# Expert layer of an eight-layer transformer: capped logits in four column strips, expert choice from them, and more gathered rows added ahead

## What is computed

```python
logits = x @ wg.T
logits = SOFTCAP * jnp.tanh(logits / SOFTCAP)          # SOFTCAP = 30
probs = jax.nn.softmax(logits, axis=-1)
topk_vals, topk_ids = jax.lax.top_k(probs, TOP_K)      # TOP_K = 2
topk_w = topk_vals / jnp.sum(topk_vals, axis=-1, keepdims=True)
route = zeros.at[arange(T)[:, None], topk_ids].set(topk_w)
h1 = jnp.einsum('th,eih->tei', x, w1);  h3 = jnp.einsum('th,eih->tei', x, w3)
out = jnp.einsum('teh,te->th', einsum('tei,ehi->teh', gelu(h1) * h3, w2), route)
```

## Time and profile before

| | |
|---|---|
| median of 3 runs | 1297.35 us (1296.9 to 1300.2) |
| the profiled execution | 1297.6 us, its span 1295.9 us (1.7 us lie around it) |
| busy shares | PE 90%, DVE 63%, ACT 51%, POOL 40% |
| mean granted TensorE clock | 0.935 |
| head, first logit product to first product of block 0 | 773.0 to 800.5 us |
| loop and spreading | 800.5 to 1022.6 us |
| DVE's last instruction of the layer | starts at 1027.9 us |

### The profile page before, as it was taken

The page is one execution under the profiler, slowest core; times in us unless marked ns, Lnnn a source line. Parts: engine busy times, 40 slices in busy tenths (PEclk is TensorE's granted clock), DMA queues, the critical chain, the costliest instruction groups (busy, mean ns, idle before and its releaser), DMA issues. The chain is left out here.

```text
span 1295.9 us, 23722 instructions
## 1 busy us (share of the span) xinstructions
PE 1161.5 (90%) x8549; PEld 882.3 (68%) x8549; DVE 816.3 (63%) x1970; ACT 664.2 (51%) x1543; POOL 513.2 (40%) x527
## 2 busy tenths in 40 slices
PE   3999999999999779777999974999999589999877
PEld 2777777777777527555677763888888467777545
DVE  6655555645644344676787755766666567777686
ACT  3344544455554332225667641666666157766575
POOL 1355654556555300028788863010000541461132
PEclk9999999999999879787999975999999879999997
DMA  7000000000000115130011024999995360000000
GB/s 194 1 14 12 3 11 13 1 13 1 1 1 1 36 42 159 39 97 23 24 33 38 12 93 142 374 379 378 366 333 181 101 174 14 16 12 2 2 8 22
DMA packets 81459, 109.03 MB, mean 84 GB/s; under 512 B 9664, under 2 KB 57168, under 8 KB 81344
## 3 DMA queue, kind: packets, MB, share of 16 engines
q1 hardware_dynamic: 79568, 102.93, 24.5%
q0 software_dynamic: 1776, 4.59, 1.2%
HBM read 102.91 MB, written 4.59 MB: 83 GB/s over the span
## 5 line engine op out<-in xcount | busy, mean ns | idle before, releaser
L907 POOL TENSOR_SCALAR a_arena<-a_arena 112x487 f32<-112x487 f32 x128 | 192.7, 1517 | 175.4 <-DVE a_arena L1124 175.4
L1213 ACT ACTIVATE a_arena<-banks,a_arena 112x487 f32<-112x487 f32 x128 | 84.3, 663 | 192.0 <-DVE a_arena L1118 192.0
L1118 DVE TENSOR_REDUCE a_arena<-banks 112x2 f32<-112x974 f32 x64 | 75.0, 1172 | 100.0 <-PE banks L995 100.0
L397 POOL TENSOR_TENSOR a_arena<-a_arena 112x375 f32<-112x375 f32 x128 | 114.5, 920 | 24.2 <-ACT a_arena L704 24.0
L513 PE MATMUL banks<-ident,a_arena 112*126 112x112 f32 x768 | 106.2, 275 | 12.8 <-POOL a_arena L397 10.3
L513 PEld LDWEIGHTS banks<-ident,a_arena 112*126 112x126 f32 x768 | 77.6, 144 | 47.3 <-issue 27.3
L2094 DVE TENSOR_TENSOR f_up_low<-f_arena,f_up_high 128x1024 fp32r<-128x1024 f32 x80 | 95.8, 1219 | 9.6 <-ACT f_up_high L2266 9.6
L712 ACT COPY a_arena<-banks 126x336 f32<-126x336 f32 x128 | 56.1, 438 | 72.8 <-PE banks L513 72.8
L2266 ACT CAST f_up_high<-f_arena 128x1024 fp32r<-128x1024 f32 x84 | 84.2, 1056 | 8.4 <-DMA f_arena<-in_L_ffn_w1T 7.8
L2150 POOL DMA_INDIRECT f_arena<-f_rows,f_arena x21 | 20.2, 961 | 171.1 <-PE banks L2188 156.8
L93 PE MATMUL banks<-a_wv_high,a_kvT_high 128*122 128x512 f32 (+1 forms) x224 | 85.6, 382 | 1.9 <-DVE a_kT_low L1070 1.9
(11 more groups left out here) (345 smaller groups left out, 2914.9 us busy)
## 6 DMA issues: line engine op xcount, KB each, us to landing
f_arena<-in_L_ffn_w1T SPq DMA_DIRECT2D x42, 512.0 KB, 7.8
f_arena<-in_L_ffn_w3T SPq DMA_DIRECT2D x42, 512.0 KB, 8.9
f_arena<-in_L_ffn_w2T SPq DMA_DIRECT2D x21, 1024.0 KB, 9.7
a_arena<-in_ctxT SPq DMA_DIRECT2D x24, 375.0 KB, 5.5
a_arena<-in_ctx SPq DMA_DIRECT2D x16, 375.0 KB
f_y<-f_arena SPq DMA_DIRECT2D x19, 128.0 KB, 7.6
a_arena<-in_L_xattn_Wkv SPq DMA_DIRECT2D x2, 1024.0 KB, 10.0
a_arena<-in_fside_BxSxS SPq DMA_DIRECT2D x8, 164.1 KB, 2.3
```

What stands on the lines that cost most here:

```text
L397: op = pool.tensor_tensor(z, z, gp[u], ALU.mult)
L907: pool.tensor_scalar(z, z, inv[:, n % 4, s:s + 1], None, ALU.mult).then_inc(p_ready, 1)
L1118: dve.tensor_reduce(negmax[:, n % 4, :], banks[0:T, 0:2, 0:KEYS], AX, ALU.max, negate=True).then_inc(max_ready, 1)
L1213: act.activation(prob[n % PR][s][:, 0:KEYS], banks[0:T, s, 0:KEYS], ACT.Exp, bias=negmax[:, n % 4, s:s + 1], accum_out=total[:, n % 4, s:s ...
```

## The change

The gate weights become the stationary operand, padded with zeros to 32 columns; 224 rows of x move past them in each of four column strips of PE, so that logits stand with experts on partitions. Tanh works on these strips (128 x 224). Eight transposes of 32 x 112 bring the capped logits back into four PSUM banks (32 columns for each group, 8 of them used). The two largest are found from the capped logits. The weights come from their difference: with e = exp(second - first), they are 1 / (1 + e) and e / (1 + e); they are made behind the token numbers. In the return four groups are added ahead instead of two, and `gathered(b + 4)` stands behind `returned(b)` and ahead of the statistics.

```diff
-        self.psL = ps[0:T, 0:B * E].rearrange("p (b e) -> p b e", e=E)
+        self.psL = ps[:, 0:R // 4]
+        self.capped = turned[0:T, :, 0:2 * STRIP].rearrange("t q (h e) -> t q h e", h=2)[:, :, :, 0:E]
...
+        pool.memset(self.wg[:, :, E:STRIP], 0.0).then_inc(s, 1)
...
         pe.wait_ge(self.s_loaded, 16)
-        for b in range(B):
-            for k in range(DC):
-                mm = pe.matmul(self.psL[:, b, :], self.xT[:, k, b * T:(b + 1) * T], self.wg[:, k, :],
-                               start=(k == 0), stop=(k == DC - 1))
+        pe.wait_ge(self.s_consts, self.CONSTS)
+        for k in range(DC):
+            for q in range(4):
+                mm = pe.matmul(self.psL[STRIP * q:STRIP * q + STRIP, :], self.wg[:, k, :],
+                               self.xT[:, k, R // 4 * q:R // 4 * (q + 1)], start=(k == 0), stop=(k == DC - 1))
         mm.then_inc(self.s_l_ready, 1)
+
+    def tensor_capped(self, pe):
+        pe.wait_ge(self.s_strips_done, 1)
+        for h in range(2):
+            for q in range(4):
+                rows = slice(STRIP * q, STRIP * q + STRIP)
+                mm = pe.transpose(self.turned[0:T, q, STRIP * h:STRIP * h + STRIP], self.strips[rows, h * T:h * T + T],
+                                  self.st["ident"][rows, rows])
+        mm.then_inc(self.s_capped_done, 1)
...
-        act.activation(self.capped, self.psL, ACT.Tanh, scale=1.0 / CAP).then_inc(self.s_capped_done, 1)
+        act.activation(self.strips, self.psL, ACT.Tanh, scale=1.0 / CAP).then_inc(self.s_strips_done, 1)
         act.wait_ge(self.s_shifted_done, 1)
-        act.activation(self.e, self.shifted, ACT.Exp, scale=CAP).then_inc(self.s_e_done, 1)
+        act.activation(self.top, self.apart, ACT.Exp, scale=CAP).then_inc(self.s_exp_done, 1)
...
-        stepped(dve.tensor_reduce(self.max, self.capped, AX, ALU.max))
-        settle()
-        dve.tensor_tensor(self.shifted, self.capped, wide(self.max), ALU.subtract).then_inc(self.s_shifted_done, 1)
-        dve.wait_ge(self.s_e_done, 1)
-        stepped(dve.tensor_reduce(self.sum, self.e, AX, ALU.add))
-        settle()
-        stepped(dve.reciprocal(self.inv, self.sum))
-        settle()
-        stepped(dve.tensor_tensor(self.p, self.e, wide(self.inv), ALU.mult))
-        for k, (p, eq, w) in enumerate(((self.p, self.eq1, self.w1), (self.p2, self.eq2, self.w2))):
-
+        for k, (p, eq, w) in enumerate(((self.capped, self.eq1, self.w1), (pairs(self.p2), self.eq2, self.w2))):
+
+            if k:
+                settle()
+            stepped(dve.tensor_reduce(self.best[:, k, :].rearrange("t (q h) -> t q h", h=2), p, AX, ALU.max))
             settle()
-            stepped(dve.tensor_reduce(self.best[:, k, :], p, AX, ALU.max))
-            settle()
-            stepped(dve.tensor_tensor(eq, p, wide(self.best[:, k, :]), ALU.is_equal))
+            stepped(dve.tensor_tensor(pairs(eq), p, pairs(wide(self.best[:, k, :])), ALU.is_equal))
             settle()
             stepped(dve.tensor_tensor(w, eq, self.rev, ALU.mult))
...
-                stepped(dve.scalar_tensor_tensor(self.p2, self.one[:, 0], -2.0, self.p, ALU.mult, ALU.add))
+                for h in range(2):
+                    stepped(dve.scalar_tensor_tensor(pairs(self.p2)[:, :, h], pairs(self.one[:, 0])[:, :, h], -4.0,
+                                                     p[:, :, h], ALU.mult, ALU.add))
         dve.tensor_tensor(self.sel[:, 0:B, :], self.one[:, 0], self.one[:, 1], ALU.add).then_inc(self.s_sel_made, 1)
-        stepped(dve.tensor_tensor(self.top, self.best[:, 0, :], self.best[:, 1, :], ALU.add))
-        settle()
-        stepped(dve.reciprocal(self.itop, self.top))
-        settle()
-        stepped(dve.tensor_tensor(self.best, self.best, self.itop.unsqueeze(1).to_broadcast([T, 2, B]), ALU.mult))
-        settle()
-        dve.tensor_scalar(self.best, self.best, self.st["tanh_g"][0:T, self.gate:self.gate + 1], None, ALU.mult
-                          ).then_inc(self.s_weighted, 1)
+        dve.tensor_tensor(self.apart, self.best[:, 1, :], self.best[:, 0, :], ALU.subtract).then_inc(self.s_shifted_done, 1)
...
         dve.tensor_scalar(self.token, self.token_f, -1.0, 0.0, ALU.add, ALU.max).then_inc(self.s_token_made, 1)
+        dve.wait_ge(self.s_exp_done, 1)
+        stepped(dve.tensor_scalar(self.first[:, 0, :], self.top, 1.0, None, ALU.add))
+        settle()
+        stepped(dve.reciprocal(self.best[:, 0, :], self.first[:, 0, :]))
+        settle()
+        stepped(dve.tensor_tensor(self.best[:, 1, :], self.best[:, 0, :], self.top, ALU.mult))
+        settle()
+        dve.tensor_scalar(self.best, self.best, self.st["tanh_g"][0:T, self.gate:self.gate + 1], None, ALU.mult
+                          ).then_inc(self.s_weighted, 1)
...
+    AHEAD = 4
...
-            gathered(0)
-            gathered(1)
+            for b in range(AHEAD):
+                gathered(b)
             for b in range(B):
-                if b + 2 < B:
-                    gathered(b + 2)
                 returned(b)
+                if b + AHEAD < B:
+                    gathered(b + AHEAD)
                 if b:
                     dve.wait_ge(finished, b)
                     follow.row(dve, b - 1)
```

More of the change, by code:

```diff
@@ L1759, with __init__ @@
 CAP = 30.0
+STRIP = 32
 class Assignment:
-    def __init__(self, m, st, xT, wgT, ps, size, blocks, late, gate=6):
+    def __init__(self, m, st, xT, wgT, ps, turned, size, blocks, late, gate=6):
         self.wgT, self.xT, self.st, self.gate = wgT, xT, st, gate
@@ L1786, in place @@
             return view
-        (self.capped, self.shifted, self.e, self.p, self.eq1, self.w1, self.p2, self.eq2, self.w2,
-         self.base) = (place(B, E) for n in range(10))
+        (self.eq1, self.w1, self.p2, self.eq2, self.w2, self.base) = (place(B, E) for n in range(6))
         self.over, self.before_more, self.picked = place(E, self.spans - 1), place(E, E), place(2, B, E)
@@ L1792, in __init__ @@
         assert self.at <= scratch.shape[1]
-        self.wg = m.sb("r_wg", [P, DC, E])
+        self.wg = m.sb("r_wg", [P, DC, STRIP])
+        self.strips = m.sb("r_strips", [P, R // 4])
         self.one = m.sb("r_one", [T, 2, B, E])
@@ L1800, in __init__ @@
         self.sel = m.sb("r_sel", [T, B + 1, E], BF16)
-        self.top, self.itop, self.max, self.sum, self.inv = (m.sb(f"r_{n}", [T, B]) for n in (
-            "top", "itop", "max", "sum", "inv"))
+        self.top, self.apart = m.sb("r_top", [T, B]), m.sb("r_apart", [T, B])
         self.best, self.first = m.sb("r_best", [T, 2, B]), m.sb("r_first", [T, 2, B])
@@ L1823, in __init__ @@
          self.s_slot_weighted) = (m.sem(f"r_{n}") for n in (
-             "loaded", "consts", "l_ready", "capped_done", "shifted_done", "e_done", "step", "sel_made", "counted",
+             "loaded", "consts", "l_ready", "capped_done", "shifted_done", "strips_done", "step", "sel_made", "counted",
              "expert_made", "hot_made", "listed", "token_made", "slot_made", "weighted", "parts_made", "weights_listed",
              "slot_weighted"))
+        self.s_exp_done = m.sem("r_exp_done")
         self.hot = None
     def sync(self, sp):
-        sp.dma_start(self.wg[:], self.wgT.rearrange("(c p) e -> p c e", p=P)).then_inc(self.s_loaded, 16)
+        sp.dma_start(self.wg[:, :, 0:self.E], self.wgT.rearrange("(c p) e -> p c e", p=P)).then_inc(self.s_loaded, 16)
     def gpsimd(self, pool):
@@ L1919, in vector, with pairs @@
         dve.wait_ge(self.s_consts, self.CONSTS)
+        def pairs(c):
+            return c.rearrange("t (q h) e -> t q h e", h=2)
         dve.wait_ge(self.s_capped_done, 1)
[L1921 to L1930 removed]
+        for k, (p, eq, w) in enumerate(((self.capped, self.eq1, self.w1), (pairs(self.p2), self.eq2, self.w2))):
+            if k:
+                settle()
+            stepped(dve.tensor_reduce(self.best[:, k, :].rearrange("t (q h) -> t q h", h=2), p, AX, ALU.max))
             settle()
[L1933 to L1935 removed]
+            stepped(dve.tensor_tensor(pairs(eq), p, pairs(wide(self.best[:, k, :])), ALU.is_equal))
             settle()
@@ L2057, in sparse_ffn @@
         st["powered"] = 0
-        routing = Assignment(m, st, xT, io["L2_ffn_wgT"], psY, SIZE, BLOCKS, LATE)
+        routing = Assignment(m, st, xT, io["L2_ffn_wgT"], psY, st["banks"][:, 0:4, :], SIZE, BLOCKS, LATE)
         routing.hot = gel_place[0:T, :].bitcast(BF16)[:, 0:2 * B * SIZE].rearrange("t (n s) -> t n s", n=2 * B)
@@ L2230, in _ @@
             routing.tensor_logits(pe)
+            routing.tensor_capped(pe)
             routing.tensor_count(pe)
```

5 lines of the change are left out of this document (3 added, 2 removed).

## The result

| | before | after |
|---|---|---|
| median of 21 runs each | 1297.06 us (1293.2 to 1302.3) | 1293.6 us (1289.8 to 1297.2) |
| ratio after / before | | 0.9969, 95% interval 0.9958 to 0.9979 |
| profiled execution | 1297.6, span 1295.9 | 1292.26, span 1290.5 |

By the ratio the change saves 4.0 us (2.7 to 5.4), 0.31%; the two medians lie 3.5 us apart.

The account below looks back on a forecast made before the run. PE bounds the loop, busy for 199.47 of 199.5 us; only the layer's ends could move. Head -2.0 plus return +1.1 gave -0.9 us, about 1296.4 us; range 1294.4 to 1298.9.

Parts of the forecast that it names:

- Logits, tanh, transposes: Head: logits in side-by-side strips 1.6 + 0.2 us, tanh 0.36 behind ACT's cast, DVE starting between 777.9 and 779.1.
- Rival (a): Head, PE: the strips run one after another, `sel` at 785.0, head gains only 0.2; 1298.2 us; chance 0.08.
- The choice: Head, DVE up to `sel`: two-SBUF-tensor steps wait for POOL's instructions; `sel` ends at 783.2, a gain of 2.0 us.
- rival (d): Head: POOL does not hold up DVE's steps; gain 2.9 to 4.1 us, 1294.3 to 1295.5; chance 0.07.
- The rule cited in the forecast: Head: VectorE instructions with two SBUF inputs contend with GpSimd SBUF readers, others do not; gain 2.0 us, without it 1.2.
- Weights, constants: Head: moving the weights behind the token numbers (0.87 us), POOL's new memset and PE's new wait cost nothing.
- The return: Layer's end, DVE: in-order waits for pairs 5, 6 and 7 leave more work behind the last gather; 1.1 us lost.
- the other bound: Return at the layer's end: a gain of 0.9 us if no pair ever waited for its gathers.
- The loop is a rigid block: Expert layer's loop, PE-bound for 199.47 of 199.5 us: untouched, it only starts and ends earlier or later with the head.
- I add +-1 us for it and no mean: PE's clock rises after two restarts: a shifted rise costs 0.5 us per us, taken as +-1 us of spread.
- its lower end, 1294.4: Bottom of the forecast range, from cases where POOL does not delay DVE or the return gains its full 0.9 us.

Follow-up runs that it names:

- e5_pool_late: Changed kernel with half of POOL's low-part work on block 0 moved behind the first two gathers, nothing left out; 1295.36 us, 0.9985 of before.
- second measurement: The changed kernel itself, unedited, measured again beside before on another chip; 1294.21 us, 0.9975 (0.9963 to 0.9987).
- third trace of after: Profile of the unedited changed kernel, from the slowest of 12 executions in its repeat beside before; 1299.6 us, their median 1294.2.
- filler kernels: Before and after, each with seven or three readerless PE products added ahead of the next layer's work; 1297.58 and 1302.62 (before), 1297.60 and 1294.14 us (after).
- w4_fill3_before: Kernel before with three readerless 512-column PE products added at the start of the next layer; 1302.62 us, 1.0031 of before.
- w3_fill3_after: Changed kernel with three readerless 512-column PE products added at the start of the next layer; 1294.14 us, 0.9968 of before.
- The two delays: Changed kernel with an idle DVE multiplication of about 1.1 or 2.2 us at the expert layer's end; 1300.11 and 1298.67 us, both 1.0007 of before.
- d1_delay: Changed kernel with an idle DVE multiplication of about 1.1 us at the end of the expert layer; 1300.11 us, 1.0007 of before.

## Why the prediction was right, and where it failed

**Logits, tanh, transposes: right.** 1.72 us against 1.6 + 0.2 forecast; tanh behind the cast, 0.35 against 0.36; transposes side by side, DVE 3.95 us behind the first product, 4.9 forecast at the early end. Rival (a), strips in a row, is out.

**The choice: right in kind, a little short.** DVE's steps with two SBUF tensors do wait for POOL's instruction, and those that read PSUM don't: with POOL moved or writing they take 0.22 us and the head falls from 9.8 to 7.7. That is also rival (d)'s price, 2.1 us, shown by `e5_pool_late`. The rule cited in the forecast, the Trainium skill's page "SBUF — State Buffer", section "Who interferes with whom", agrees with these rows for readers on POOL (0.61 to 1.18 us against 0.22, and 0.22 and 0.14 for the steps with a PSUM input). In two of the three traces the gain is 2.3 to 2.4 us instead of 2.0 (the third, with 10.22, gains 2.0), because ACT's cast ended 0.7 us sooner after the first product (3.11 us, 3.78 before). Of the 0.95 us by which DVE started sooner than forecast, 0.5 went into its waits for POOL: 5.81 us to the end of `sel`, 5.3 forecast.

**Weights, constants: right.** Nothing waits for them; the distance from `sel` to the loop is the same (15.30 us before, 15.46 after).

**The return: right.** Three waits at the forecast pairs, +1.08 us against +1.13. On the first chip, where the spreading came late and the gathers had landed ahead of it, the new order gains 0.9 instead (10.19 to 9.28), which was the other bound.

**"The loop is a rigid block": nearly.** In two of three traces, and in five of the variants with the new head, it is 0.5 us shorter, because the clock rises 3.2 instead of 4.2 us behind its first product (after: 0.50 from 798.90 to 799.40, then 0.99 to 799.90; before). In the third it rises after 6.2 us, and the loop takes 217.84.

**"I add +-1 us for it and no mean": the step that failed.** The clock was counted at two restarts only, as noise around layers that would move as a whole. The runs show that unchanged code moves too. In the first two traces of after, head -2.3, loop -0.5, return +1.1, with small rests, make this layer 1.8 us shorter; the next layer gives another 1.4 without an edit, and the last takes 0.5. That is -2.7, at the edge of the measured -2.7 to -5.4 and inside the second measurement's -1.7 to -4.8. Of the 1.8 us between the forecast and -2.7, 0.9 are the next and last layers, 0.5 the loop and 0.4 the head with the small rests. What remains up to 4.0 is not resolved by single traces. With the third trace of after, whose loop, next and last layers are longer, the mean is only -1.2. For this layer the first two are the usual case: the filler kernels, which have the same code up to its end, take 261.43 and 261.13 us there with the new head, and 263.30 and 263.39 with the old.

The range had a gap of its own: its upper end had the clock in it (rival (a)'s 1298.2 became 1298.9), its lower end, 1294.4, had not. With 1 us for it the lower end would have been 1293.4, below the 1293.6 measured; that would have met the number without the mechanism, since a mean for the layers behind was still missing.

**What is shown, and what is open.** Shown: the code behind the change, unedited, takes from 190.7 to 193.6 us in the next layer and from 72.7 to 78.3 in the last; the next layer's time goes with the place of its second rise; the first rise does not set it; three fillers at the start of that layer raise the total by 4.0 us in one kernel and not in the other (`w4_fill3_before`, `w3_fill3_after`). The two delays point the same way, but with one trace each, and with the four unchanged layers ahead moving by 6 us from trace to trace, they do not separate the effect of a shift from what a program does by itself. Only argued: that it is a shift that makes the next layer 1.4 us shorter in after, and not another difference of the two programs; for it speaks that the four layers ahead take the same time within 0.5 us in five of the six traces of before and after (322.4 in the sixth, which is longer behind as well), and that each trace with a later rise is longer, whatever its edit. Open: what puts the second rise at 29 or 31 or 35 us, and the last layer at 73, 75.5 or 78 us; both were only seen, not steered; and why the third trace of after, with the same code, had its rise at 30.8. Not tried: a delay ahead of the expert layer.

## What to carry to other kernels

Where PE is the bound and its clock falls and rises within a layer, the layers behind an edit can come out several us longer or shorter without an edit of their own (up to 3 us in the next and 5 in the last here): keep a range for it on both sides, measure pieces by landmarks in several traces of each kernel, and don't read one span difference as the edit's price. An order of waits that takes its data in sequence must have as few steps as possible behind the last arrival, and what is queued there counts more than idle time filled ahead. Beside a chain of small DVE steps, look for long POOL instructions that read SBUF: moved past the chain they gave the head 2.1 us here, which did not show in the total alone (0.9985), and may be part of the 0.9943 measured, in six executions, together with the return's repair.

## What the runs showed of the hardware that was not expected

- In 20 traces, the last layer took 72.7 to 73.9, about 75.5 or about 78.2 us, with nothing between. The next layer, without fillers, took 190.7 to 193.6. One program, `d1_delay`, showed two groups of times 6 us or more apart.
- Three filler products that run in PE's idle time and have no reader cost 4.0 us of total in one kernel and gained nothing in the other, although they doubled the granted clock for the first real work.
